# The queries' rope moves from GpSimd to VectorE in an attention and mixture-of-experts kernel

## The reference

```python
xn = _layernorm(x)
# attention: 16 heads of 16, causal
q = _apply_rope((xn @ Wq + bq).reshape(B, S, H, D), cos, sin)
k = _apply_rope((xn @ Wk + bk).reshape(B, S, H, D), cos, sin)
attn = softmax(where(causal, -inf, einsum('bshd,bthd->bhst', q, k) / sqrt(D)))
attended = einsum('bhst,bthd->bshd', attn, v).reshape(B, S, E) @ Wo + bo
# experts: the best 6 of 64 for each row, and two shared ones; silu(g) * u, 176 wide
routed = sum over the 6 of weight * ((silu(xn @ Wg.T) * (xn @ Wu.T)) @ Wd.T)
x = x + attended + routed + shared
```

## Time and profile before

| | us |
|---|---|
| runs shown, median (lowest to highest) | 649.49 (647.65 to 653.19) |
| profiled execution, its own time | 650.96 |
| its span, first to last instruction | 649.1 |
| TensorE busy in the span | 615.3 |
| VectorE busy | 430.5 |
| GpSimd busy | 321.0 |

### The profile page before, as it was taken

How to read it: one execution, slowest core, us unless ns; L and a number is a source line. 1 busy time by engine, 2 the same in 40 slices (tenths; PEclk the granted TensorE clock), 3 DMA queues, 4 the chain that set the end, 5 groups by cost and what they waited for, 6 DMA issues and landing times.

```text
span 649.1 us, 17796 instructions
## 1 busy us (share of the span) xinstructions
PE 615.3 (95%) x4929; PEld 364.3 (56%) x4929; DVE 430.5 (66%) x1366; ACT 307.2 (47%) x802; POOL 321.0 (49%) x340
## 2 busy tenths in 40 slices
PE   6999999998998999998999999999999899999987
PEld 3644455654554555554555555555554566666654
DVE  6768688557664665667665565544446788899865
ACT  3643131033443444444444544444445777777752
POOL 4000000268636775567765686564300776766662
PEclk9999999999997999999999999999999999999999
DMA  9610011138978768996799977996425777777432
GB/s 297 179 30 2 0 34 34 57 103 255 283 228 278 232 190 247 320 334 185 213 298 295 315 222 235 327 327 134 102 59 193 210 232 229 227 227 232 129 109 74
DMA packets 78167, 124.52 MB, mean 192 GB/s; under 512 B 11113, under 2 KB 52618, under 8 KB 78090
## 3 DMA queue, kind: packets, MB, share of 16 engines
q1 hardware_dynamic: 43098, 60.18, 30.4%
q0 software_dynamic: 15872, 46.16, 24.4%
q10 hardware_dynamic: 19120, 17.18, 7.8%
HBM read 85.73 MB, written 37.75 MB: 190 GB/s over the span
## 4 chain that ended last, share of the span: by engine, by line
PE 80%; DVE 6%; DMA 3%; issue 3%; ACT 3%; POOL 2%; DVEq 1%; SPq 0%; ACTq 0%; POOLq 0%
PE pair L1216 23%; PE pair L1243 14%; PE pair L1186 6%; PE pair L1173 5%; PE pair L1121 4%; PE bank L1227 4%; PE bank L1330 4%; PE bank L1200 3%; PE bank L1362 2%; PE pair L1083 2%; DVE negm L985 2%; DMA lower<-xn_rows,idx_all 2%; PE pair L1292 2%; PE pair L1312 1%; PE bank L1341 1%
## 5 line engine op out<-in xcount | busy, mean ns | idle before, releaser
L454 POOL DMA_INDIRECT lower<-xn_rows,idx_all x128 | 138.0, 1078 | 221.8 <-DVE idx_all L958 107.8
L1216 PE MATMUL pair<-space,work 128*64 (+1 forms) x768 | 167.4, 467 | 6.3 <-DVE wqkv_sb L932 3.7
L1243 PE MATMUL pair<-lower,work 88*64 x512 | 121.5, 379 | 0.7 <-ACT lower L615 0.7
L1216 PEld LDWEIGHTS pair<-space,work 128*64 128x64 f32 x768 | 67.4, 138 | 78.4 <-issue 66.9
L874 DVE TENSOR_TENSOR work<-work,pair 128x176 f32<-128x176 f32 x128 | 42.9, 337 | 101.5 <-ACT work L609 100.7
L1243 PEld LDWEIGHTS pair<-lower,work 88*64 88x64 f32 x512 | 69.6, 137 | 48.7 <-issue 18.0
L1216 PE MATMUL pair<-wqkv_sb,work 128*64 128x352 f32 x256 | 90.6, 477 | 0.0
L615 ACT ACTIVATE lower<-pair 128x256 f32<-128x256 f32 x128 | 49.1, 384 | 76.5 <-PE pair L1243 76.5
L519 POOL DMA_INDIRECT wqkv_sb<-y_rows,slot_i x48 | 48.1, 1002 | 58.2 <-DVE negm L985 33.2
L602 ACT ACTIVATE work<-pair 128x256 f32<-128x256 f32 x128 | 42.6, 381 | 66.9 <-PE pair L1173 41.3
L985 DVE TENSOR_REDUCE negm<-pair 128x2 f32<-128x256 f32 (+1 forms) x128 | 64.6, 549 | 9.5 <-PE pair L1292 7.5
(11 more groups left out here) (205 smaller groups left out, 1156.5 us busy)
## 6 DMA issues: line engine op xcount, KB each, us to landing
space<-wgu SPq DMA_DIRECT2D x66, 352.0 KB
y_rows<-lower ACTq DMA_DIRECT2D x128, 128.0 KB, 4.3
qk_all<-qk_rows SPq DMA_DIRECT2D x64, 256.0 KB
lower<-wdn SPq DMA_DIRECT2D x64, 176.0 KB
qk_rows<-qk_all POOLq DMA_DIRECT2D x32, 256.0 KB, 5.7
qk_rows<-space POOLq DMA_DIRECT2D x16, 256.0 KB, 4.0
xn_rows<-qk_all SPq DMA_DIRECT2D x16, 128.0 KB, 1.9
lower<-xn_rows,idx_all POOLq DMA_INDIRECT x128
```

Of the source, the lines that this page charges most:

```text
L454: po.indirect_dma_start(xg[:, r % XB, :], None, xn_rows[:, :], bass.IndirectOffsetOnAxis(idx_all[:, r:r + 1], 0)).then_inc(xg_in[r % XB], 16)
L1216: last = pe.matmul(pair[u % 2][strip, 0:2 * F], xgT[u][:, c, strip], n, start=c == 0, stop=c == EC - 1, skip_group_check=True)
L1243: last = pe.matmul(pair[u % 2][strip, 512:512 + E], hT[:, u % 2, c, strip], n, start=c == 0, stop=c == 1, skip_group_check=True)
```

## The change

VectorE makes all 72 steps, the queries' too (`turn_keys` becomes `turn_piece`, with `a` for queries or keys). A piece takes six turns in place of nine, in turns 1 to 48, with one, two, one, two, one and two steps in them. One semaphore, `turned_ok`, counts all steps. GpSimd keeps the gathers and the stores: the eight stores of piece n follow gathers 24 + 12n to 31 + 12n, one behind each, the first waiting for the piece's ninth step. The stores, their sources and their sizes are the same. GpSimd no longer waits for projections or tables before its first gather.

```diff
-PIECE_STEPS = ROPE_STEPS + 2 * COPIES
+PIECE_TURNS = 6
+STORES_FROM = 2 * PIECE_TURNS + 12
...
             def piece(n, j):
                 g, a, u = n // 2, n % 2, n % BUFS
-                if k >= ROPE_STEPS:
-                    i, x = (k - ROPE_STEPS) // 2, (k - ROPE_STEPS) % 2
-                    if k == ROPE_STEPS:
-                        po.wait_ge(turned_ok if a else roped, ROPE_STEPS * (n // 2 + 1))
...
-                if k < 2:
-                    i = po.tensor_tensor(batches(other[:, k]), batches(q[:, 1 - k]), sin, ALU.mult)
-                elif k < 4:
-                    i = po.tensor_tensor(batches(q[:, k - 2]), batches(q[:, k - 2]), cos, ALU.mult)
...
+                i, x = j // 2, j % 2
+                if j == 0:
+                    po.wait_ge(turned_ok, ROPE_STEPS * (n + 1))
+                src = spare[u] if i in HIGH_IN[a] else qT[:, g, a]
...
             for r in range(RT):
                 gather(r)
-                while r >= XB and r % 2 and done < (r - XB + 1) * todo // (RT - 4 * XB) and done < todo:
-                    piece(*steps[done])
-                    done += 1
+                n, j = (r - STORES_FROM) // (2 * PIECE_TURNS), (r - STORES_FROM) % (2 * PIECE_TURNS)
+                if 0 <= n < PIECES and j < 2 * COPIES:
+                    piece(n, j)
...
-            def turn_keys(n, k):
-                g, u = n // 2, n % BUFS
-                q, other = qT[:, g, 1], spare[u]
-                if n > 1 or k:
-                    dve.wait_ge(turned_ok, ROPE_STEPS * (n // 2) + k)
+            def turn_piece(n, k):
+                g, a, u = n // 2, n % 2, n % BUFS
+                q, other = qT[:, g, a], spare[u]
+                if n or k:
+                    dve.wait_ge(turned_ok, ROPE_STEPS * n + k)
...
-                if 0 < i // 2 <= PIECES // 2 * ROPE_STEPS:
-                    turn_keys((i // 2 - 1) // ROPE_STEPS * 2 + 1, (i // 2 - 1) % ROPE_STEPS)
+                n, j = (i // 2 - 1) // PIECE_TURNS, (i // 2 - 1) % PIECE_TURNS
+                if 0 <= n < PIECES:
+                    for k in range(j * ROPE_STEPS // PIECE_TURNS, (j + 1) * ROPE_STEPS // PIECE_TURNS):
+                        turn_piece(n, k)
```

More of the change, by code:

```diff
@@ L279, in build @@
         w_loaded = [sem("w_loaded_even"), sem("w_loaded_odd")]
-        gu_own = sem("gu_own"); dn_own = sem("dn_own"); idx_col = sem("idx_col"); po_turn = sem("po_turn"); roped = sem("roped"); turned_ok = sem("turned_ok");
+        gu_own = sem("gu_own"); dn_own = sem("dn_own"); idx_col = sem("idx_col"); turned_ok = sem("turned_ok");
         table_set = sem("table_set"); table_at = sem("table_at"); bias_at = sem("bias_at"); bias_ok = sem("bias_ok"); tables_in = sem("tables_in")
@@ L455, in gather, with piece @@
                                       bass.IndirectOffsetOnAxis(idx_all[:, r:r + 1], 0)).then_inc(xg_in[r % XB], 16)
-            def piece(n, k):
+            def piece(n, j):
                 g, a, u = n // 2, n % 2, n % BUFS
-                q, other = qT[:, g, a], spare[u]
-                if k >= ROPE_STEPS:
-                    i, x = (k - ROPE_STEPS) // 2, (k - ROPE_STEPS) % 2
-                    if k == ROPE_STEPS:
-                        po.wait_ge(turned_ok if a else roped, ROPE_STEPS * (n // 2 + 1))
[L465 to L479, removed]
-                if k < 2:
-                    i = po.tensor_tensor(batches(other[:, k]), batches(q[:, 1 - k]), sin, ALU.mult)
-                elif k < 4:
-                    i = po.tensor_tensor(batches(q[:, k - 2]), batches(q[:, k - 2]), cos, ALU.mult)
[L485 to L493, removed]
@@ L495, in _ @@
-            po.wait_ge(qkv_ok, len(order))
-            po.wait_ge(tables_in, 1)
+                i, x = j // 2, j % 2
+                if j == 0:
+                    po.wait_ge(turned_ok, ROPE_STEPS * (n + 1))
+                at = qk_rows.rearrange("(h i x d) a t -> h i d x a t", h=H, i=COPIES, x=2)
+                src = spare[u] if i in HIGH_IN[a] else qT[:, g, a]
+                po.dma_start(at[:, i, :, x, a, g * SPAN_T:(g + 1) * SPAN_T], src[:, x]).then_inc(rows_out[u], 16)
             po.wait_ge(idx_ok, 1)
@@ L498, in _ @@
             po.wait_ge(xn_out, 16 * NT)
-            steps = [(n, k) for n in range(PIECES) for k in range(ROPE_STEPS if n % 2 else 0, PIECE_STEPS)]
-            todo = len(steps)
-            done = 0
             for r in range(RT):
                 gather(r)
-                while r >= XB and r % 2 and done < (r - XB + 1) * todo // (RT - 4 * XB) and done < todo:
-                    piece(*steps[done])
-                    done += 1
-            assert done == todo
+                n, j = (r - STORES_FROM) // (2 * PIECE_TURNS), (r - STORES_FROM) % (2 * PIECE_TURNS)
@@ L898, in turn_keys @@
                     dve.wait_ge(rows_out[u], 16 * 2 * COPIES * (n // BUFS))
-                cos, sin = (table[:, 1, cs].unsqueeze(1).to_broadcast([P, SPAN_T // S, S]) for cs in range(2))
+                cos, sin = (table[:, a, cs].unsqueeze(1).to_broadcast([P, SPAN_T // S, S]) for cs in range(2))
                 def batches(z):
```

## The result

The changed kernel takes 654.26 us (median of nine runs, 653.08 to 655.55), the kernel before 650.69 beside it (nine runs, 647.35 to 653.19): a ratio of 1.0072 with a 95% interval of 1.0049 to 1.0094. It is slower by 0.7%; the forecast was 653.0, of a range from 646 to 659. The profiled execution took 653.91 around a span of 652.0, 2.9 us more than before.

What follows compares the result with a forecast made beforehand. TensorE, busy 95%, was taken to bound the kernel with a floor of 5.275 us a turn. The terms -14.6 + 17.5 + 0.35 + 0.9 = +4.1, less perhaps 0.6, gave +3.5: 653.0 us, range 646 to 659.

Steps and rivals of the forecast that it cites:

- The two-step turn: Routed-stage turns with two VectorE steps: weight copy 0.86 us later, 0.76 beyond the slack; 23 turns cost 17.5 us.
- The rival in which the chain runs ahead: VectorE's queue: register instructions before the copy run despite the second step's wait; 0.62 us a turn, total 649.5; chance 0.20.
- The rival of the hidden step: Routed stage: TensorE's wait for the copy is off the path in uncontended turns, only gains stay; 635 us; chance 0.06.
- The gains: Five long stretches of the routed stage lose TensorE's stalls once GpSimd drops the queries' rope; 14.6 us in all.
- 2.6 left as they are: Excess over the floor in twenty turns between the long stretches, not counted as gain; perhaps 0.6 us of it vanishes.
- The stall of the keys' stores: GpSimd at 187 to 195 holds gathers back 7.86 us, TensorE's clock falls; removing it gains 5.9 us.
- The overlap with GpSimd: GpSimd's rope arithmetic stretches VectorE copies and steps beside it; pieces 2, 4 and 6 gain 5.3 us when it goes.
- The loss: Routed stage: added VectorE steps delay TensorE by 17.5 + 0.35 us, later register loads by 0.9.
- The 24th turn: Last turn with two VectorE steps: no slot weights there, which gives back 0.41 us, so it costs 0.35.
- The register loads: VectorE's two expert-number loads start later in turns with two steps and delay the next hidden products; about 0.9 us.
- The register loads as a bound: VectorE's two loads lengthen to 2.3 us together, hidden products come 0.4 later in 24 turns; 662 us; chance 0.14.
- The gather that takes the port first: Copies on VectorE wait up to 1.1 us for a GpSimd gather in 24 turns; 679 us; chance 0.03.

Runs made afterwards that it cites:

- the kernel without the inner wait: Changed kernel with a piece's steps paired so that the second of two steps in a turn doesn't wait for the first; 647.39 us, ratio 0.9978.
- the kernel with two places: Changed kernel with the first of a turn's two steps moved between the up-weight and down-weight copies; 638.16 us, ratio 0.9852.
- the one-step kernel: Changed kernel with the second step of each two-step turn left out (24 of 72 not computed); 637.53 us, ratio 0.9836.
- the idle products: Changed kernel without second steps in a turn, plus 36 unused 128x512 products on GpSimd at the queries' old steps; 650.93 us, ratio 1.0041.
- fills: Changed kernel without second steps in a turn, plus three unused 128x512 GpSimd fills at each of the queries' 36 old steps; 656.94 us, ratio 1.0121.

## Why the prediction was right, step by step

**The two-step turn** (forecast 0.76, measured 0.76 to 0.77 in 13 of them). Each part came out: second step 0.72 after the first (0.72), copy 0.74 after that (0.75), no slack but the 0.10. The choice that decided it was the register chain: here it doesn't run while the step ahead of it waits. The sequencer's records show that in after (first instruction at 188.926, second step at 188.911), and the kernel without the inner wait shows it by taking the wait away. The rival in which the chain runs ahead had a price of 0.62 a turn; that kernel, in which it does, has mostly 0.50 to 0.66, though with the steps 0.60 apart and not 0.72, and it gives 647.4, where the rival was put at 649.5.

**The place on the path.** The rival of the hidden step (635) fell with the changed kernel, and the kernel with two places shows how near it was: it gives 638.2 by moving 24 instructions behind two copies. The forecast priced the steps at the place where the change puts them; that the price belongs to the place, the experiment adds.

**The gains** (forecast 14.6, plus 2.6 left as they are). Measured 13.6 in the stage by the one-step kernel, against the whole 17.2. The first turns lost their stall: no wait for gathers, no copy above 0.57 there. The stall of the keys' stores was worth what it was put at. The overlap with GpSimd is confirmed in kind; its size alone was not measured, since the idle products cost more than the steps that they stand for. Mis-sized is the 2.6: in the changed kernel only 0.5 is left beside the two-step turns, where I let 0.6 of it vanish. The one-step kernel still has 3.6 of small stalls, so these are not due to GpSimd's rope. Of its nine turns with a step that are over by more than 0.1, seven are ones that carry two steps in after, and there TensorE waits for the copy anyway; that they vanish for this reason fits, but was not tested.

**The loss** (forecast 17.5 + 0.35 + 0.9 = 18.75, less 0.6). Measured 19.5 in the two-step turns, 16.2 against the one-step kernel. The 24th turn was put at 0.35 and measured 0.71: the register chain was done at 416.48, but the copy started at 416.88. The table names a weight transfer for these 0.40; the copy's three waits had been met by then in the queue's records, and the turn from 172.88 has the same 0.40 between two instructions of the chain (177.76 to 178.16), named "issue" (the row of 178.35). Elsewhere such a pause is 0.05, so the sum lacked 0.35 in each of these two turns, 0.7 in all. Nine more turns were over by 0.80 to 0.92. In those the copy starts in time and TensorE goes on 0.97 to 1.09 after it in place of 0.93. The records of TensorE's queue show where: its register instructions between the met wait and the first up product have a pause that is 0.04 to 0.16 longer (0.26 in place of 0.11 from 269.60 to 269.86); in the turn from 366.06 the copy itself also takes 0.59. The sum had no term for pauses in a queue, which cost wherever the chain is exposed; together they are some 1.5 of the 19.5. What causes them stays open. The register loads (forecast 0.9, though 0.17 x 24 x 0.2 gives 0.8) delayed one turn after a two-step turn by 0.28. The queue ahead of them starts later, but the loads themselves became shorter, with a median of 0.44 in place of 0.58.

**The other rivals.** The register loads as a bound (662) would have shown hidden products later than 3.0 us after the up products; one turn of 48 has that (394.82, 3.14). The gather that takes the port first (679) would have shown copies above 0.6: the means are 0.525 and 0.527, the longest of the 128 is 0.61, and the copy of 201.70 takes 0.53 inside a gather that began at 201.32. The rule of the Trainium skill behind that rival (SBUF — State Buffer, "Who interferes with whom") lets whichever issues first hold the shared port pair, while the other blocks. For these gathers the trace doesn't agree. That copies are held beside GpSimd's products and fills it does show, but not the order: the copy of 156.22 in the earlier trace rows starts 0.30 ahead of GpSimd's subtraction (156.52 to 157.80) and is held all the same until that is over, so 1.97 does not bear the rule out as the prediction says.

The net was +3.5 in the forecast and +3.6 between the medians. That the two agree so closely is partly luck: the loss in the two-step turns was 0.8 above its terms, the small stalls that vanished were 1.5 above theirs, and the stage began 0.5 late.

## What to carry to other kernels

Price an operation that moves to another engine by the loop it lands on and the slack of that loop, not by the engine's busy share: VectorE was a third idle, and 24 steps of 0.69 us cost 16 us in one place of its queue and at most 0.6 in another. Put added work behind the last instruction in a turn that the bounding engine waits for. Where one instruction must wait for the one ahead of it, count what stands behind it in the queue too: its wait holds back register and address instructions that would otherwise have run in its shadow, 0.14 us here, on top of the 0.12 that the two instructions lose in overlap.

## What the hardware showed that was not expected

A pause of 0.38 to 0.43 us in VectorE's instruction queue, between two register instructions or ahead of the copy, with no wait in the records to explain it (177.76 to 178.16, 416.48 to 416.88). It has a place in the program: counted over all records of VectorE, ten of the eleven such pauses ahead of a register instruction in the routed stage of after stand at the 63rd or 64th of every 128 (178.16, 241.64, 263.59, 285.70 and on), and those of the kernel before and of the one-step kernel stand there or one record beside it. Under other work it is harmless (one falls into the turn from 281.43, which takes 5.27); it costs 0.35 when the chain is on the path. TensorE's longer pauses are as regular: eight of the nine turns that have them lie six turns apart (161.53, 195.85, 229.84 and on). No run here shows what the queues do then.

Three fills in a row on GpSimd take 2.40 us beside VectorE's conversion and copies (0.55, 0.96 and 0.78 and the pauses between them), while the shortest single fills take 0.52: the copy and the fill hold each other up, in both directions.

In the table of waits 14.0 us of TensorE's waits carry the name of a ScalarE operation, and these waits end 0.93 to 1.09 us after a VectorE copy begins. Counting the semaphore's updates, or an experiment that moves VectorE's instructions alone, settles whose they are.
